# Inner chunks of a feed-forward network in groups of three, with the next tokens split at the head of a unit

## The reference

```python
dispatch = flat[order]                       # 8 experts, their best tokens, 64 units of 490 in the kernel
gate = jax.nn.silu(jnp.einsum('ech,ehi->eci', dispatch, w1))
up = jnp.einsum('ech,ehi->eci', dispatch, w3)
expert_out = jnp.einsum('eci,eih->ech', gate * up, w2) * weight_sel[..., None]
routed = routed.at[order.reshape(-1)].add(expert_out.reshape(-1, h))
shared = jax.nn.silu(flat @ s1) * (flat @ s3) @ s2      # every one of the 12544 tokens
out = routed + shared                        # h is 192, i is 768
```

## Time and profile before

| | us |
|---|---|
| median of 3 runs | 3433.06 (3431.37 to 3438.18) |
| the profiled execution | 3431.96 |
| its span, first to last instruction | 3430.2 |
| PE busy | 3138.3, 91% of the span |
| DVE, ACT, POOL busy | 2433.1, 1557.6, 1373.6 |

### The profile page before, as it was taken

One profiled execution on the slowest core, in us unless ns is written; L12 is line 12 of the kernel. 1 busy time (PEld: TensorE's weight loads), 2 busy tenths in 40 slices (PEclk: granted clock), 3 DMA queues, 4 the chain that ended last, 5 costly groups with the idle time before them and its releaser, 6 DMA issues. The chain is left out here.

```text
span 3430.2 us, 72008 instructions
## 1 busy us (share of the span) xinstructions
PE 3138.3 (91%) x26164; PEld 2153.2 (63%) x26164; DVE 2433.1 (71%) x4832; ACT 1557.6 (45%) x3287; POOL 1373.6 (40%) x1170
## 2 busy tenths in 40 slices
PE   6999999999999999998129999989999999999997
PEld 5777777777777777766125555556565566566664
DVE  6999999999999999997655555555545455455543
ACT  2445444544454454543004444444555455455543
POOL 1322233223322332222205555036665565556664
PEclk9899999999999999985559999999999999999999
DMA  3333233323332333322111222234554545445443
GB/s 105 74 74 80 69 86 84 75 64 86 88 74 67 81 87 74 75 44 54 44 52 48 77 67 72 74 91 76 98 95 71 99 76 97 92 73 101 75 73 42
DMA packets 461611, 260.21 MB, mean 76 GB/s; under 512 B 339103, under 2 KB 442879, under 8 KB 457183
## 3 DMA queue, kind: packets, MB, share of 16 engines
q1 hardware_dynamic: 393632, 196.42, 24.0%
q0 software_dynamic: 54400, 49.00, 10.0%
q10 hardware_dynamic: 13262, 10.66, 0.9%
HBM read 107.98 MB, written 68.15 MB: 51 GB/s over the span
## 5 line engine op out<-in xcount | busy, mean ns | idle before, releaser
L1270 DVE SCALAR_TENSOR_TENSOR ffn_hidden<-ffn_up,ffn_silu 128x490 f32<-128x490 f32 (+2 forms) x534 | 350.6, 670 | 690.2 <-ACT ffn_silu L1251 653.7
L689 POOL TENSOR_TENSOR weights<-weights,x_pair 128x400 f32<-128x400 f32 x384 | 395.3, 1029 | 830.6 <-DVE weights L561 819.6
L1251 ACT ACTIVATE ffn_silu<-ffn_gate 128x490 f32<-128x490 f32 (+2 forms) x534 | 301.5, 582 | 722.8 <-PE ffn_up L1214 722.4
L1440 POOL DMA_INDIRECT out_rows<-done,ids x256 | 408.2, 1594 | 401.2 <-ACT done L1542 339.7
L613 DVE RECIPROCAL recip<-x_product 128x200 f32<-128x200 f32 x384 | 534.8, 1393 | 0.0
L1235 PE MATMUL ffn_out<-ffn_w_hi,ffn_hidden_hi 128*128 128x192 f16 (+1 forms) x2124 | 525.3, 247 | 2.2 <-DVE ffn_hidden_lo L1263 1.8
L1237 PE MATMUL ffn_out<-ffn_w_hi,ffn_hidden_lo 128*128 128x192 f16 (+1 forms) x2124 | 522.5, 246 | 0.0
L1236 PE MATMUL ffn_out<-ffn_w_lo,ffn_hidden_hi 128*128 128x192 f16 (+1 forms) x2124 | 522.5, 246 | 0.0
L747 PE MATMUL bank<-w_tok,patches 128*128 128x192 f32 x1536 | 342.8, 383 | 39.2 <-DVE minus_half L525 24.1
L1263 DVE TENSOR_TENSOR ffn_hidden_lo<-ffn_hidden,ffn_hidden_hi 128x490 f16<-128x490 f32 (+2 forms) x534 | 356.5, 668 | 16.2
L1245 ACT CAST ffn_hidden_hi<-ffn_hidden 128x490 f16<-128x490 f32 (+2 forms) x534 | 320.7, 601 | 85.7 <-DVE ffn_hidden L1270 85.7
(11 more groups left out here) (176 smaller groups left out, 6934.4 us busy)
## 6 DMA issues: line engine op xcount, KB each, us to landing
patches<-in_patches SPq DMA_DIRECT2D x32, 1176.0 KB, 5.3
ffn_raw<-in_w SPq DMA_DIRECT2D x18, 768.0 KB
dram_x_t<-x_t SPq DMA_DIRECT2D x32, 392.0 KB, 3.7
x_t<-dram_x_t SPq DMA_DIRECT2D x24, 512.0 KB, 5.4
base<-dram_h SPq DMA_DIRECT2D x24, 384.0 KB, 4.2
out_rows<-sums ACTq DMA_DIRECT2D x24, 384.0 KB, 4.7
v_held<-v SPq DMA_DIRECT2D x64, 102.0 KB, 2.3
dram_h<-h SPq DMA_DIRECT2D x32, 192.0 KB
```

Of the source, the lines that this page charges most:

```text
L689: nc.gpsimd.tensor_tensor(weights[:, n % 4], weights[:, n % 4], x_pair[:, n % 4, ::-1], ALU.mult)\
L1251: nc.scalar.activation(T.silu[:, m % 2, 0:n], T.gate[m % 2][:, 0:n], ACT.Silu, scale=1.0 / (TOKEN_SCALE * WEIGHT_SCALE)).then_inc(T.silued, 1)
L1270: nc.vector.scalar_tensor_tensor(T.hidden[:, m % 2, 0:n], T.up[m % 2][:, 0:n], HIDDEN_SCALE / (TOKEN_SCALE * WEIGHT_SCALE), T.silu[:, m % ...
L1440: nc.gpsimd.indirect_dma_start(out=dram["out"][:, :], out_offset=bass.IndirectOffsetOnAxis(ap=ids[i][0:height, t, 0:1], axis=0), in_=done[ ...
```

## The change

Chunks go in two groups of three, with three banks each for gate and for up, so that all eight banks of PSUM are used. Before chunk m PE waits for the product of chunk m-3. The output products of the unit before follow in halves. `split_at` is None in all units: the split of the next unit's tokens stands ahead of the first silu on ACT and ahead of the first product on DVE. Nothing is added or left out; SP's and POOL's programs are the same.

```diff
+GROUP = 3
+PARTS = MI // GROUP
-        [ctx.enter_context(nc.psum_tensor(f"ffn_{name}{b}", [128, 512], F32)) for b in range(2)]
-        for name in ("gate", "up", "out"))
+        [ctx.enter_context(nc.psum_tensor(f"ffn_{name}{b}", [128, 512], F32)) for b in range(banks)]
+        for name, banks in (("gate", GROUP), ("up", GROUP), ("out", 2)))
...
-def tensor_pair(nc, pe, T, g, slot, ws, n, pair):
+def tensor_group(nc, pe, T, g, slot, ws, n, group):
+    chunks = range(GROUP * group, GROUP * group + GROUP)
...
-    for m in (2 * pair, 2 * pair + 1):
-        pe.wait_ge(T.multiplied, MI * g + m + 1)
+    for m in chunks:
+        if not (isinstance(g, int) and g == 0 and m == 0):
+            pe.wait_ge(T.multiplied, MI * g + m)
...
-        for out, hi, lo in ((T.gate[m % 2], T.w_hi[ws][0], T.w_lo[ws][0]), (T.up[m % 2], T.w_hi[ws][1], T.w_lo[ws][1])):
+        for out, hi, lo in ((T.gate[m % GROUP], T.w_hi[ws][0], T.w_lo[ws][0]), (T.up[m % GROUP], T.w_hi[ws][1], T.w_lo[ws][1])):
...
-    share = len(tiles) * MI // 3
-    for k in range(third * share, (third + 1) * share):
+    share = len(tiles) * MI // PARTS
+    for k in range(part * share, (part + 1) * share):
...
+    if split_at is None:
+        split()
     for m in range(MI):
         act.wait_ge(T.gated, 2 * (MI * g + m + 1))
...
+    if split_at is None:
+        split()
     for m in range(MI):
         dve.wait_ge(T.silued, MI * g + m + 1)
...
-                scalar_unit(nc, act, T, g, slot, columns_of(tiles), split_next, 1 if tiles is SHORT else 3)
+                scalar_unit(nc, act, T, g, slot, columns_of(tiles), split_next, None)
...
-                scalar_unit(nc, act, T, g, 1 - i % 2, XU, split_next, 1)
+                scalar_unit(nc, act, T, g, 1 - i % 2, XU, split_next, None)
...
-                vector_unit(nc, dve, T, g, slot, columns_of(tiles), split_next, 1 if tiles is SHORT else 3)
+                vector_unit(nc, dve, T, g, slot, columns_of(tiles), split_next, None)
...
-                vector_unit(nc, dve, T, g, 1 - i % 2, XU, split_next, 1)
+                vector_unit(nc, dve, T, g, 1 - i % 2, XU, split_next, None)
```

More of the change, by code:

```diff
@@ L1209, in tensor_pair, with tensor_out @@
             nc.tensor.matmul(out, hi[:, beyond], far, start=False, stop=False)
-    for m in (2 * pair, 2 * pair + 1):
+    for m in chunks:
         beyond = slice(INNER + m * 128, INNER + (m + 1) * 128)
-        nc.tensor.matmul(T.gate[m % 2][:, 0:n], T.w_lo[ws][0][top, beyond], far[top], start=False, stop=True)\
+        nc.tensor.matmul(T.gate[m % GROUP][:, 0:n], T.w_lo[ws][0][top, beyond], far[top], start=False, stop=True)\
           .then_inc(T.gated, 1)
-        nc.tensor.matmul(T.up[m % 2][:, 0:n], T.w_lo[ws][1][low, beyond], far_again[low], start=False, stop=True)\
+        nc.tensor.matmul(T.up[m % GROUP][:, 0:n], T.w_lo[ws][1][low, beyond], far_again[low], start=False, stop=True)\
           .then_inc(T.gated, 1)
-def tensor_out(nc, pe, T, g, slot, ws, tiles, third):
-    if third == 0:
+def tensor_out(nc, pe, T, g, slot, ws, tiles, part):
+    if part == 0:
         pe.wait_ge(T.lo_ready, MI * g + MI + 2)
@@ L1250, in scalar_unit @@
         act.wait_ge(T.multiplied, MI * g + m + 1)
-        nc.scalar.activation(T.silu[:, m % 2, 0:n], T.gate[m % 2][:, 0:n], ACT.Silu,
+        nc.scalar.activation(T.silu[:, m % 2, 0:n], T.gate[m % GROUP][:, 0:n], ACT.Silu,
                              scale=1.0 / (TOKEN_SCALE * WEIGHT_SCALE)).then_inc(T.silued, 1)
@@ L1269, in vector_unit @@
         dve.wait_ge(T.lo_ready, MI * g + m + 1)
-        nc.vector.scalar_tensor_tensor(T.hidden[:, m % 2, 0:n], T.up[m % 2][:, 0:n],
+        nc.vector.scalar_tensor_tensor(T.hidden[:, m % 2, 0:n], T.up[m % GROUP][:, 0:n],
                                        HIDDEN_SCALE / (TOKEN_SCALE * WEIGHT_SCALE), T.silu[:, m % 2, 0:n],
@@ L1480, in unit @@
                 pe.wait_ge(T.tokens_lo, 2 * g + 6)
-                for part in range(3):
-                    tensor_pair(nc, pe, T, g, slot, 0, columns_of(tiles), part)
+                for part in range(PARTS):
+                    tensor_group(nc, pe, T, g, slot, 0, columns_of(tiles), part)
                     if not (isinstance(g, int) and g == 0):
@@ L1493, in routed @@
                 pe.wait_ge(tokens_in[1 - i % 2], 64 * half + 64)
-                for part in range(3):
-                    tensor_pair(nc, pe, T, g, 1 - i % 2, ws, XU, part)
+                for part in range(PARTS):
+                    tensor_group(nc, pe, T, g, 1 - i % 2, ws, XU, part)
                     if opening(e, i):
```

## The result

The changed kernel takes 3547.20 us (median of 4 runs, 3545.67 to 3551.30) against 3435.62 for the kernel before, run beside it: a ratio of 1.0325, 95% interval 1.0306 to 1.0345. The forecast was 3540, slower, with a range of 3507 to 3565; sign and range hold. The clock was taken 13 us too low, and other terms gave 6 of these back.

A forecast was written before the change was run, and what follows sets the result against it. PE was taken to bound the kernel. From 3431.96 profiled, +98.5 (shared units' standstill) + 24 (clock) - 12.8 (routed units) - 2 (unit 0) = +107.7 gave 3539.7, forecast 3540, range 3507 to 3565.

The forecast's parts named there:

- unit without the clock: Shared units 2 to 22: second group at S (first matmul) + 13.79, plus 9.01, makes 22.80, 4.57 more than 18.23.
- the clock, a unit: Shared units: PE's standstill of about 4.6 lowers the granted clock, costing 0.8 x 1.35 = 1.1 a unit, 24 in all.
- unit 23: Shared unit whose next load is half as wide: it stands about 2.5, plus 1.1 for the clock.
- routed stage, sum: The 64 routed units: larger groups gain 0.2 each, 12.8 in all; the split at the head costs nothing there.
- unit 24: Change from shared to routed stage: PE already waits for gathered rows; this stretch stays unchanged, +-2.
- beginning: Unit 0, with no output products to hide behind, loses one of its gaps: 2 us less.
- The chain of the standstill: Shared units: late x_t holds ACT's split, then DVE's split and first product, so PE's second group stands 4.8.
- The fit that the prediction gives: Load of x_t: about 2.0 us plus bytes over 436 GB/s, 3.2 for 512 KB; the sum would be some 48 less.
- 2.7 of busy time at 0.50: Clock step: in the earlier trace an idle stretch of 7.90 was followed by this low clock, 1.35 lost.
- That the clock holds: Rival for the shared units: the clock holds through the idle stretches, 24 less, 3516; chance 0.24.
- the other side: Rival: x_t is there by S + 4.85, only the shorter PE path is left, 20 less, 3412, faster; chance 0.06.
- That the load lands sooner: Rival for shared units: each microsecond x_t lands earlier takes 22 off; 2 us less gives 3496; chance 0.06.

The follow-up runs named there:

- early load: The changed kernel, but SP issues x_t(g+1) ahead of its wait for base(g), one unit earlier: 3407.93 us, ratio 0.993 to the kernel before.
- fill: The changed kernel, but in shared units PE makes the first half of the output products twice: 3516.23 us, ratio 1.0244 to the kernel before.
- swapped loads: The changed kernel, but SP issues x_t(g+1) just ahead of base(g), behind the same wait: 3501.55 us, ratio 1.0197 to the kernel before.

## Why the prediction held, and where it was off

| step | predicted | measured, mean of units 2 to 22 |
|---|---|---|
| x_t issued | S + 4.23 | S + 4.30 |
| ACT's split begins | S + 9.63 | S + 9.53 |
| DVE's last split instruction | S + 12.32 | S + 12.21 |
| PE's second group | S + 13.79 | S + 13.68 |
| unit without the clock | 22.80 | 22.70 (13.68 + 9.02) |
| the clock, a unit | 1.1 | 1.75 (24.45 - 22.70) |
| unit 23 | +2.5 and 1.1 | +2.4, no low clock |
| routed stage, sum | -12.8 | -15.5 |
| unit 24 | 0 | +0.8 |
| beginning | -2 | -3.8 |

- **The chain of the standstill** was right at every step. From the split on it is 0.1 a unit early: the load was issued 0.07 later than predicted, and the split began 5.23 behind the issue where 5.40 were taken; the loads landed in 5.1 in the median and not in 5.4. The early load shows its cause: with the load a unit earlier the wait is gone. The fit that the prediction gives from the Trainium skill (DMA: Bandwidth & Descriptors, Anatomy of one DMA — SWDGE (gpsimd) path) is one for DMAs that GpSimd issues. SP issues these, so its 3.2 us is no measure for them; the shortest landing in the shared stage here is 4.6.
- **The clock** is the term of the sum that was mis-sized: 1.75 x 21 = 36.8 instead of 24, 13 more. The step that was off is "2.7 of busy time at 0.50", 1.35 lost, times a chance of 0.8: a fall of the clock came in 21 of 21 units and cost 1.75. The stretch of the earlier trace rows was the end of a longer one: in the trace of before the clock was at 0.50 already in the idle time ahead of it,

```profile
2242.60:2246.70 4.10, 0.00 (x0) 0.00 (x0) 4.10 (x6) 0.02 (x1) 2.33 (x2) 0.50 0.14 25
```

so 2.7 was what a long wait had left over, not what a drop costs. After the change all 21 waits (4.04 to 4.81) were followed by low clock, 17 times for 3.41 and 4 times for 6.83, most of it busy time; a stretch of 3.41 that is busy throughout loses 3.41 x 0.5 = 1.7.
- **The routed stage** gave its 0.21 a unit, 17.74 to 17.53, as costed; nothing there became late. The 2.7 beyond it are mostly the first routed unit (15.67 to 14.56) and two others at a turn of the expert's loop (21.22 to 20.32, 20.74 to 20.17), which had been left out of the sum. The beginning gained 1.8 more than was taken. Of that 1.1 lies ahead of unit 0, whose start differs by up to 3.7 in the ten traces (1791.99 to 1795.65), so this part may be scatter; the rest is in units 0 (2.5 for the 2 taken) and 1 (0.2).
- **The rivals.** That the clock holds was priced at 3516; in the changed kernel it held in none of the 21 units. The fill, which makes it hold by added work, ran at 3516.2. The 3412 of the other side needed a load issued a unit earlier, which this kernel does not have; with it 3407.9 were measured. That the load lands sooner was priced at 22 for each microsecond; with the swapped loads PE's second group starts 1.19 a unit sooner and the span is 43.8 shorter, since fewer drops of the clock come on top.

Sum of the errors: -2 (chain, 21 x 0.1), +13 (clock), -3 (routed), +1 (unit 24) and -2 (beginning) make the 7 by which the profiled execution (3546.5) lay above 3539.7. That the forecast came so near is in part luck: the 13 of the clock were halved by errors of the other sign that have nothing to do with it.

## What to carry to other kernels

A step that is moved ahead in an engine's program takes its inputs' deadlines with it: look up when its transfer is issued and what that issue waits for, and move the load by as much as the step. The Trainium skill's rule for this (DMA: Bandwidth & Descriptors, Rules for kernel authors), to issue a DMA early and to wait for it late, was the point on which this change turned: with groups of three the same split lost 3.2% with the late load and won 0.7% with the early one. A larger group needed a moved split, and a split at the head needed the larger group and an earlier load; in shared units a place behind chunk 2 did as well without moving the load. The groups alone (0.6% slower) and the split alone (6.2% slower) both lost, so the parts of such a change are worth a run of their own.

## What the runs showed of the hardware that was not expected

The granted clock behind a wait of PE, one wait in each of the units 2 to 22:

| kernel | length of the waits | followed by low clock | unit beyond its path |
|---|---|---|---|
| groups, split behind chunk 3 | 1.06 to 1.07 | 0 of 21 | |
| pairs, head, early load | 1.53 to 1.89 | 0 of 21 | |
| fill | 1.23 to 2.20 | 1 of 21 | 0.1 |
| swapped loads | 2.69 to 4.00 | 13 of 21 | 1.05 |
| the change | 4.04 to 4.81 | 21 of 21 | 1.75 |
| pairs, head, late load | 7.00 to 7.57 | 21 of 21 | 1.76 |

Length alone does not decide it: 2.97 came twice, once with and once without. A wait of 7 costs no more clock than one of 4.5, because half of its low stretch (6.83) passes while PE is idle anyway. The windows of one such wait and of the busy time behind it:

```profile
2116.25:2123.40 7.15, 0.00 (x0) 0.00 (x0) 2.08 (x4) 2.86 (x5) 3.36 (x4) 0.77 0.34 114
2123.46:2126.90 3.44, 3.44 (x9) 1.24 (x10) 1.23 (x2) 0.60 (x1) 2.83 (x3) 0.50 0.02 1
```

And giving PE 36 matmuls a unit that nobody needs made the kernel some 28 us faster (83.2 for 111.6 over the kernel before), which is the cheapest way seen here to price the clock.
